# Setup reordered, the router's bias added on VectorE, its logits in another PSUM bank, down_w loaded behind up_w, and the slots' instructions put in another order

## The reference

```
mod = (silu(c) @ wmod).reshape(32, 6, 1, -1)          # sa, ca, ga, sb, cb, gb
ga, gb = sign(g) * max(|g|, 0.25)
h = layernorm(x) * (1 + ca) + sa
x = x + ga * (scan(h) @ W.T + b + conv5(h) + conv_b)
h = layernorm(x) * (1 + cb) + sb
sel = argmax(gelu(h[:, -1] @ Wp1 + bp1) @ Wp2 + bp2)
y = gelu(h @ W1[sel] + b1[sel]) @ W2[sel] + b2[sel]
x = x + gb * (h + 0.3 * (y @ Wo + bo))
```

## Time and profile before

| what | value |
|---|---|
| runs | 662.33, 667.11, 666.33 us; median 666.33 |
| profiled execution | 664.8 us |
| its span on the core | 662.8 us |
| TensorE busy | 640.0 us (97%) |
| VectorE, ScalarE, GpSimd busy | 561.0, 562.2, 447.6 us (85, 85, 68%) |
| granted TensorE clock, mean | 0.996 |
| moved by DMA | 120.58 MB, mean 182 GB/s |

### The profile page before, as it was taken

The page is one execution under the profiler, slowest core; times in us unless marked ns, Lnnn a source line. Parts: engine busy times, 40 slices in busy tenths (PEclk is TensorE's granted clock), DMA queues, the critical chain, the costliest instruction groups (busy, mean ns, idle before and its releaser), DMA issues.

```text
span 662.8 us, 11162 instructions
## 1 busy us (share of the span) xinstructions
PE 640.0 (97%) x3469; PEld 526.8 (79%) x3469; DVE 561.0 (85%) x863; ACT 562.2 (85%) x976; POOL 447.6 (68%) x536
## 2 busy tenths in 40 slices
PE   6988999999999999999999999999999999999986
PEld 6877778888888878888888888888888878888765
DVE  1697889999999989999999999999999989998612
ACT  3788688889988888888998889888899889887753
POOL 2885476876667666777676766778776766666543
PEclk9999999999999999999999999999999999999999
DMA  8999546665555554665454555566555445555551
GB/s 288 357 349 319 162 128 192 191 186 149 156 159 180 159 183 167 192 192 179 124 194 149 182 161 186 164 191 191 189 143 153 150 167 188 160 159 159 159 158 65
DMA packets 55454, 120.58 MB, mean 182 GB/s; under 512 B 5643, under 2 KB 43364, under 8 KB 46180
## 3 DMA queue, kind: packets, MB, share of 16 engines
q1 hardware_dynamic: 51844, 115.65, 54.9%
q10 hardware_dynamic: 3552, 4.23, 2.1%
HBM read 61.12 MB, written 25.19 MB: 130 GB/s over the span
## 4 chain that ended last, share of the span: by engine, by line
PE 82%; DMA 8%; ACT 3%; DVE 3%; issue 2%; POOL 1%; SPq 1%; DVEq 0%; ACTq 0%
PE U L1051 10%; PE U L1053 8%; PE U L1052 8%; PE Q L1071 8%; PE TR L1091 8%; PE Q L1066 8%; PE Q L1067 8%; DMA up_w<-up_table 5%; PE Q L1083 4%; PE Y L1035 4%; PE Y L1031 4%; PE Y L1032 4%; PE TR L1083 4%; PE Q L1016 2%; DMA xr<-in_L_ffn_W_dram 2%
## 5 line engine op out<-in xcount | busy, mean ns | idle before, releaser
L454 POOL TENSOR_TENSOR g_lo<-g,g_hi 128x512 fp32r<-128x512 f32 x128 | 169.8, 1329 | 151.5 <-ACT g_hi L614 149.4
L835 DVE SCALAR_TENSOR_TENSOR Y<-h,taps,Y 128x512 f32<-128x512 f32 x320 | 222.4, 750 | 3.2 <-PE Y L1035 0.9
L1051 PE MATMUL U<-hid_hi,up_w 128*128 128x512 f32 x256 | 110.1, 430 | 4.7 <-DMA up_w<-up_table 3.7
L1066 PE MATMUL Q<-g_hi,down_w 128*128 128x512 f32 x256 | 103.7, 405 | 0.3 <-issue 0.3
L566 ACT ACTIVATE S<-xr,nmr,rstd 128x256 f32<-128x256 f32 x128 | 66.6, 591 | 42.2 <-POOL S_lo L462 40.0
L1067 PE MATMUL Q<-g_hi,down_w 128*128 128x512 f32 x256 | 101.1, 395 | 0.0
L1053 PE MATMUL U<-hid_lo,up_w 128*128 128x512 f32 x256 | 100.8, 394 | 0.0
L1052 PE MATMUL U<-hid_hi,up_w 128*128 128x512 f32 x256 | 100.6, 393 | 0.0
L783 DVE BATCH_NORM_STATS2 st<-xr 128x6 f32<-128x512 f32 x128 | 88.0, 709 | 12.8 <-DMA xr<-in_L_attn_x_dram 8.5
L880 DVE TENSOR_TENSOR_SCAN S<-keep,h 128x512 f32<-128x512 f32 x64 | 76.6, 1235 | 25.3 <-ACT h L684 25.3
L607 ACT ACTIVATE g<-U,up_w 128x512 f32<-128x512 f32 x128 | 87.2, 682 | 10.8 <-PE U L1053 10.3
(11 more groups left out here) (116 smaller groups left out, 1272.3 us busy)
## 6 DMA issues: line engine op xcount, KB each, us to landing
up_w<-up_table SPq DMA_DIRECT2D x32, 1027.0 KB, 6.6
down_w<-down_tab SPq DMA_DIRECT2D x32, 1024.0 KB, 8.6
xr<-in_L_attn_x_dram SPq DMA_DIRECT2D x32, 512.0 KB, 3.5
out_dram<-xr SPq DMA_DIRECT2D x64, 256.0 KB, 2.3
xr<-in_L_ffn_W_dram ACTq DMA_DIRECT2D x5, 512.0 KB, 10.2
xr<-in_L_ffn_W_dram SPq DMA_DIRECT2D x4, 512.0 KB, 8.9
up_table<-g_lo SPq DMA_DIRECT2D x2, 1024.0 KB, 11.8
up_table<-down_w SPq DMA_DIRECT2D x2, 1024.0 KB, 13.4
```

Of the source, the lines that this page charges most:

```text
L454: nc.gpsimd.tensor_tensor(g_lo[:, f], g[:, f % 2], g_hi[:, f].bitcast(f32), ALU.subtract).then_inc(g_lo_ready, 1)
L835: ins = nc.vector.scalar_tensor_tensor(out=Y[c][:, :], in0=h[:, c, k:k + T], scalar=taps[:, c, k:k + 1], in1=Y[c][:, :], op0=ALU.mult, op1 ...
L1051: mm(U[f % 2][:, :], up_w[:, par, UP + w:UP + w + P], hid_hi[:, par, c], start=(c == 0), stop=False)
L1066: mm(Q[c][:, :], down_w[:, par, 1, w:w + P], g_hi[:, f], start=(f == 0), stop=False)
```

## The change

- Router: the bias matmul (L1112) goes; the logits go to U[0] behind the third GELU (a new wait), VectorE adds bp2 into a small SBUF tile `logits` and searches there. `up(i, 3)` waits for nav instead of the index, and the index is waited for in `up(i, 0)` of the next slot.
- SP: `fetch` waits for up_w's landing before it issues down_w.
- TensorE's slot: xn's transposes ahead of the output's, all of up 2 ahead of `router_nav`, `down(i, 0)` behind xn1's transposes, the logits behind it, `down(i, 1)` ahead of `back_to_tokens`.
- ScalarE's slot: `hid_of` ahead of the second `g_high`, the third GELU ahead of nav, `h_of` ahead of `gate1`.
- GpSimd's slot: `norm1` right behind `norm2`, `gate_beta` ahead of the first `g_low`.
- VectorE's slot: `stats1` after two conv steps, `residual2` after seven instead of six.
- The setup's order on all five engines. On SP the wait for the modulation weights (`for_modulations`) goes, and the router's weights, W and the second W1 block are loaded earlier, the last W1 block later.

```diff
+                beta_out()
 
                 sp.wait_ge(s_w2T_mm, 4)
                 load_w1(7)
-                split_out(4)
-                load_router()
                 split_out(5)
-                beta_out()
                 split_out(6)
 
                 sp.wait_ge(s_w1_lo, E)
@@ -398,6 +394,8 @@
                 sp.dma_start(up_w[:, par].bitcast(f32), up_table[bass.ds(e, 1)].rearrange("o p n -> p (o n)")).then_inc(up_loaded[par], 16)
                 if r == 0:
                     sp.wait_ge(s_down_lo, 2 * E)
+
+                sp.wait_ge(up_loaded[par], 16 * (r // 2 + 1))
                 sp.dma_start(down_w[:, par].rearrange("p k n -> p (k n)").bitcast(f32),
                              down_tab[:, bass.ds(e, 1)].rearrange("p o k n -> p (o k n)").bitcast(f32)).then_inc(down_loaded[par], 16)
 
...
             def slot(i):
                 if row(i + 1):
                     norm2(i + 1)
+                if row(i + 4):
+                    norm1(i + 4)
                 if row(i):
+                    gate_beta(i)
                     g_low(i, 0)
-                    gate_beta(i)
                     g_low(i, 1)
                 if row(i + 1):
                     hid_low(i + 1)
-                if row(i + 4):
-                    norm1(i + 4)
                 if row(i):
                     g_low(i, 2)
                     g_low(i, 3)
                 if row(i + 3):
                     s_low0(i + 3)
...
+                w2T_copy(4)
+                down_high(3, 0)
                 w1_hi(5)
-                down_high(2, 0)
-                down_high(2, 1)
-                w2T_copy(3)
-                h_of(1)
...
                 down_high(4, 1)
                 hid_of(0)
                 w2T_copy(6)
+                w1_hi(7)
                 down_high(5, 0)
...
@@ -746,17 +745,21 @@
                     gelu(i, 0)
                     g_high(i, 0)
                     gelu(i, 1)
+                if row(i + 1):
+                    hid_of(i + 1)
+                if row(i):
                     g_high(i, 1)
                 if row(i + 1):
-                    hid_of(i + 1)
                     hid_high(i + 1)
+                if row(i):
+                    gelu(i, 2)
+                if row(i + 1):
                     nav_of(i + 1)
+                if row(i + 3):
+                    h_of(i + 3)
                 if row(i + 2):
                     gate1(i + 2)
-                if row(i + 3):
-                    h_of(i + 3)
                 if row(i):
-                    gelu(i, 2)
                     g_high(i, 2)
                     gelu(i, 3)
...
@@ -869,9 +873,13 @@
 
             def router(r):
                 dve.wait_ge(r_logits, r + 1)
-                nc.vector.max(top8[:, :], U[1][0:1, 8:8 + E]).then_inc(top_ready, 1)
+                if r == 0:
+                    dve.wait_ge(s_small, SMALL_LOADED)
+                nc.vector.tensor_tensor(logits[:, :], U[0][0:1, 8:8 + E], bp2_sb[:, :], ALU.add).then_inc(logits_ready, 1)
+                dve.wait_ge(logits_ready, r + 1)
+                nc.vector.max(top8[:, :], logits[:, :]).then_inc(top_ready, 1)
                 dve.wait_ge(top_ready, r + 1)
-                nc.vector.max_index(sel8[:, r % 2], top8[:, :], U[1][0:1, 8:8 + E]).then_inc(sel_ready, 1)
+                nc.vector.max_index(sel8[:, r % 2], top8[:, :], logits[:, :]).then_inc(sel_ready, 1)
...
                 scan(2, 1)
+                stats1(3)
+                down_low(6, 0)
+                down_low(6, 1)
+                router(0)
                 residual1(1, 0)
-                down_low(5, 1)
-                down_low(6, 0)
-                stats1(3)
-                router(0)
-                down_low(6, 1)
                 residual1(1, 1)
+                s_low1(2)
                 down_low(7, 0)
                 down_low(7, 1)
-                s_low1(2)
...
             def slot(i):
                 if row(i - 1):
                     output(i - 1)
                 if row(i + 2):
-                    conv(i + 2, 0, 6)
+                    conv(i + 2, 0, 2)
+                if row(i + 4):
+                    stats1(i + 4)
+                if row(i + 2):
+                    conv(i + 2, 2, 7)
                 if row(i - 1):
                     residual2(i - 1)
                 if row(i + 2):
-                    conv(i + 2, 6, TAPS * DC)
-                if row(i + 4):
-                    stats1(i + 4)
+                    conv(i + 2, 7, TAPS * DC)
                 if row(i + 1):
...
@@ -1040,11 +1051,11 @@
                 if f == 0:
                     pe.wait_ge(up_loaded[par], 16 * (i // 2 + 1))
                     pe.wait_ge(hid_lo_ready, DC * (i + 1))
-                if f == 1:
-                    wait(pe, sel_ready, i + 1)
+
+                    pe.wait_ge(sel_ready, i + 1)
                 if f == 3:
 
-                    pe.wait_ge(sel_ready, min(i + 2, B))
+                    pe.wait_ge(nav_ready, min(i + 2, B))
                 wait(pe, gelu_out, n - 1)
...
             def router_logits(r):
                 pe.wait_ge(nav_ready, r + 1)
-                mm(U[1][0:1, 8:8 + E], nav[:, :], wp2[:, :], start=True, stop=False)
-                mm(U[1][0:1, 8:8 + E], ident[0:1, 0:1], bp2_sb[:, :], start=False, stop=True).then_inc(r_logits, 1)
+
+                wait(pe, gelu_out, FC * (r - 1) + 3 if r else 0)
+                mm(U[0][0:1, 8:8 + E], nav[:, :], wp2[:, :], start=True, stop=True).then_inc(r_logits, 1)
...
-                w2_transposes(7)
+                comb(6, 0)
+                comb(6, 1)
                 back_to_tokens(1)
                 router_nav(0)
-                comb(6, 0)
-                comb(6, 1)
+                comb(7, 0)
                 router_logits(0)
-                comb(7, 0)
                 comb(7, 1)
...
             def slot(i):
@@ -1171,29 +1183,30 @@
                 if row(i):
                     up(i, 0)
                     up(i, 1)
+                if row(i + 1):
+                    to_channels(i + 1, xn, xn2_ready, t3_done)
                 if row(i - 1):
                     out_to_tokens(i - 1)
-                if row(i + 1):
-                    to_channels(i + 1, xn, xn2_ready, t3_done)
                 if row(i):
                     up(i, 2, (0,))
-                    down(i, 0)
+                    up(i, 2, (1,))
                 if row(i + 1):
                     router_nav(i + 1)
-                if row(i):
-                    up(i, 2, (1,))
-                if row(i + 1):
-                    router_logits(i + 1)
                 if row(i + 3):
                     to_channels(i + 3, xn1, xn1_ready, t1_done)
                 if row(i):
+                    down(i, 0)
+                if row(i + 1):
+                    router_logits(i + 1)
+                if row(i):
                     up(i, 3)
+                    down(i, 1)
                 if row(i + 2):
                     back_to_tokens(i + 2)
                 if row(i):
-                    down(i, 1)
                     down(i, 2)
                     down(i, 3)
```

129 lines of the change are left out of this document (66 added, 63 removed).

## The result

The changed kernel takes 654.42 us (median of 4 runs, 653.61 to 655.51) against 665.2 of the kernel before on the same chip; the ratio is 0.9852, with a 95% interval of 0.9819 to 0.9886. The profiled span went from 662.8 to 651.8 us.

The account below looks back on a forecast made before the run. It took TensorE's instruction stream, 18.39 us a slot, as the bound. Gains of 5.3 + 0.5 + 1.3 + 1.4 + 1.0 = 9.5 us took the profiled 664.8 to 655.3, set at 656.5 between two time scales; range 651 to 666.

Parts of the forecast that it names:

- slots: The 28 full slots (i = 1 to 28): each goes from 18.39 to 18.2 us, 5.3 us gained.
- other slots: The other slots with a router (0, 29, 30): 0.5 us gained.
- stalls: Two late up_w loads in the full slots cost 0.61 and 1.35 us; 1.3 of 1.96 comes back.
- tail: Last slots, 30 and 31: up_w lands sooner with down_w behind it, less waiting for down_w; 1.4 us gained.
- setup: Before the first slot: a W2 block load 2 to 3 us earlier, with counter-effects; 1.0 us gained, between 5 gained and 3 lost.
- ScalarE's whole program with S_lo: Loop in each slot of all ScalarE's work and VectorE's S_lo: 18.40 less the 0.25 router wait, 18.15 us.
- The hold-up of the scan by hid_lo: In each slot GpSimd's hid_lo meets VectorE's scan, which starts up to 0.1 to 0.3 us late.
- TensorE's two savings: Per slot on TensorE: 0.12 us for the bias matmul and 0.15 for up 3's wait, giving 18.12.
- the 1.0 us for down_w: In slots 30 and 31 TensorE waits for the later-issued down_w, together about 1.0 us lost.
- 1 (slot stays at 18.39): Rival for the full slots: the loop of VectorE and GpSimd takes over, 18.39 us stays; 661.8 us, chance 0.21.
- 2 (setup 4 us late): Rival: the slot shrinks, but the setup ends 4 us later through x(3) and w1_lo(7); 661.5 us, chance 0.12.
- 3 (slower): Rival: norm1 late, hid_lo holds up the first scan in full, slot 18.8 us; 674 us, chance 0.10.

Follow-up runs that it names:

- run 9: The changed kernel with SP loading x(i+5) between up_w and down_w, not ahead of up_w; 656.01 us, ratio 0.9876 to the kernel before.
- run 7: The changed kernel with ScalarE's second g_hi ahead of hid's two activations, as before; 655.07 us, ratio 0.9862 to the kernel before.
- run 5: The changed kernel with the bias as a second matmul again, in U[0], without VectorE's addition; 655.06 us, ratio 0.987 to the kernel before.
- run 3: The changed kernel with up 3 waiting for the index again in place of nav; 675.37 us, ratio 1.0168 to the kernel before.
- run 4: The kernel before with only the bias added on VectorE and up 3 waiting for that addition, not the index; 670.04 us, ratio 1.0089 to the kernel before.
- run 1: The changed kernel with the setup of before on all five engines; 654.3 us, ratio 0.9848 to the kernel before.
- run 2: The changed kernel without SP's wait for up_w, so down_w is issued at once behind it; 661.02 us, ratio 0.9966 to the kernel before.
- run 10: The changed kernel with stats1(3) behind router(0) in VectorE's setup, not ahead of down_low(6,0); 654.96 us, ratio 0.9861 to the kernel before.
- run 12: The changed kernel with VectorE's slot of before, stats1 behind all ten conv steps; 843.45 us, ratio 1.2703 to the kernel before.
- run 8: The kernel before with one added line: SP waits for up_w's landing before issuing down_w; 660.58 us, ratio 0.995 to the kernel before.
- run 6: The changed kernel with GpSimd's slot of before, norm1 behind hid's low part; 685.91 us, ratio 1.033 to the kernel before.

## Why the prediction came out right, point by point

The terms of the sum, forecast and then measured in the spans of the two traces: slots 5.3 and 6.2, other slots 0.5 and 1.5, stalls 1.3 and about 1.0, tail 1.4 and 2.3, setup 1.0 and 0.1; together 9.5 and 11.0. Each is off by 0.3 to 1.0 us, in both directions, so the sum is better than its terms.

**The slot** (forecast 18.2, bounds 18.12 and 18.8). Measured 18.18 where it is settled, 18.21 as the mean of slots 1 to 28 with the stall. The number is right, but the loop behind it is another one than I had, and that they are within 0.03 us of each other is luck. I had taken ScalarE's whole program with S_lo as the loop and put it at 18.15, by taking its 0.25 us wait for the router away from 18.40. That wait is gone, but two things were left out. First, the new order makes ScalarE's own work shorter: from xn to the end of the second S_hi, less the listed waits, it is 16.33 us instead of 16.76. One reason is that a GELU and the g_hi that reads it start 0.72 us apart where one stands right behind the other (141.45 and 142.17 before), and a GELU and the nav behind it only 0.58 (555.21 and 555.79 after). With the 1.40 for S_lo this loop would need 17.73, not 18.15. Second, stats1 now stands ahead of eight of the ten conv steps on VectorE, so that conv ends 10.6 us behind VectorE's S_lo instead of 9.5, and h stands ahead of gate1 on ScalarE; so conv's end holds the second h, gate1 and the third g_hi. That closes the loop over VectorE, ScalarE and GpSimd shown above, and its length is 18.18. The prediction had no such loop. Its pieces have the same lengths in the changed kernel and in run 9, and run 7 shows that ScalarE's part ahead of the second h is not in it; that it is the bound is read from the traces and not shown by a run that shortens it.

Two of the reasons beside it don't hold either. The hold-up of the scan by hid_lo is there (2.67 instead of 2.31), but run 7 shows that it costs nothing. And TensorE's two savings are not simply 0.12 and 0.15: the first is worth 0.06 (run 5), the second 0.72 in the order in which it now stands (run 3), and both together in the old order lose 6.5 us (run 4).

**The other slots** (0.5 for slots 0, 29, 30). Slot 0 alone gave 1.48, of which at most 0.4 came from the setup (run 1). This term was mis-sized.

**The stalls** (1.3 of 1.96 back). About 1.0 came back in the trace. But the question behind the term was wrong: I asked what the new order of loads gives back of the two stalls there were, not what stalls the shorter slot would have without it. Run 2 shows 3.2 us of waits in slots 1 to 28, where the kernel before had 1.4, and 3.4 us more time there than the changed kernel. The prediction had said that the later issue leaves less room, and named 2.0 us as the loss; that bound was for the loads in their new order.

**The tail** (1.4 gained). 2.28 gained from slot 29 on. The two waits for up_w before (0.75 at 627.64 and 1.53) became one of 0.64, which is 1.6 of it; the other 0.6 is shorter work in these slots. up_w landed after 4.92 us in slot 31, as taken; TensorE waited 0.64 for it there, so 0.9 came of the 1.5 that I had put for that slot:

```profile
633.35 0.50 PE L1062 MATMUL U<-hid_hi,up_w 128*128 128x512 f32 x1 [0.64 <-DMA up_w<-up_table]
```

The term that was wrong is the 1.0 us for down_w: I used 4.9 to 6.8 us for it, and it took 4.7, less than the 5.2 that down 0 stands behind up 0. No wait for it is in this trace. The 4.4 us that I worked out from the Trainium skill ("SBUF — State Buffer", The DMA setup-cost knee) for 1 MB lies 0.3 below that 4.7 and just below the least, 4.5; my lower bound of 4.9 lies 0.2 above it, and the upper one, 6.8, came from a load that had a neighbour.

**The setup** (1.0 gained, 5 to -3). Nothing that can be told from noise, by the trace (0.14) and by run 1. The counter-effect through x(3) was rightly named. Missing in the prediction were the late load of the last W1 block, which is what w1_lo(7) waited for, and the two paths that run 10 found beside the router's, the store of the last table block and mix.

**Rivals.** 1 (slot stays at 18.39) is out: every slot behind the first few and outside the stall is 18.11 to 18.22. 2 (setup 4 us late) is out: 75.30. 3 (slower) did not come about, but run 12 shows that its point of decision was well seen and its price, 0.4 us a slot, far too low: with norm1 late the slot is 6.6 us longer, and by another mechanism than a held-up scan. What keeps the changed kernel from it is that stats1 was moved along with norm1. GpSimd's norm1 then waits 2.42 us for its statistics in each slot, and the third g_low has 1.75 to spare.

**What decided it as a whole.** Without the change of SP's order the rest gives 0.34% (run 2), that order alone 0.5% (run 8), both 1.48%. So the terms of the sum of 9.5 us are not separable: each holds with the others in place, and none of the kernels of runs 2, 4 and 8, which have a part of the change each, is faster by over 1%.

## What to carry to other kernels

When several engines run loops of nearly one length, list the starts of one instruction per slot on each engine: the loop whose period stays constant while another's varies is the bound, and shortening anything else gives only what lies above it. Several engines show that period, so follow the loop piece by piece through the waits: an engine that waits 0.45 us for another in every slot is not a loop by itself. Redo such a loop for the new order, since moving an instruction can shorten one loop and close another. An edit that makes the slot shorter also shortens the time that each prefetch has; ask what a load would have in the new slot with its old order, not only what it waited in the old one. If a consumer is moved forward on one in-order engine, its producer has to be moved forward on the other, or everything behind the consumer stands still.

## What was not expected of the hardware

- A GpSimd instruction on 4 elements per partition takes 0.23 us and, when it begins within one of VectorE's scans, mostly 1.02 to 1.16; the power 1.04 and 1.90 to 2.06 (before, and runs 4 and 6). Beside conv steps, which work on Y in PSUM, the same instructions keep their 0.23 and 1.04. The rule of the Trainium skill cited in the prediction ("SBUF — State Buffer", Who interferes with whom) says this; I had applied it to hid_lo's large pieces only.
- The same load of 1 MB (down_w) takes 4.7 us alone and 8.6 (up to 11.1) beside another 1 MB. Both loads have landed 9.1 us behind the issue of the first when they run side by side (before), and 9.8 when one runs behind the other (run 8, medians). For that 0.7 the first is there 1.1 to 1.6 us sooner (medians 6.6 before against 5.0 in run 8, 7.3 in run 2 against 6.2 in the changed kernel).
- A stall of TensorE of 1.0 us cost 0.6 (run 9), since the loop that was the bound had waited only in part (one period of 18.78 on ScalarE), and TensorE made up the rest at 18.12 a slot.
- The first up 0 came between 73.5 and 76.6 us in profiles of kernels with one and the same setup (runs 3 and 7), so a term of 1 us in a setup with many loads can't be judged from a single profile.
